# Two receiving buffers for the transposed rows and a single pair of operands, in a mixture-of-experts tail of an fp32 transformer layer

## The reference

```python
def ffn(x, gate_w, gate_b, bias, w1, b1, w2, b2):      # x: 2048 x 512, 8 experts, H = 352
    scores = x @ gate_w.T + gate_b + bias
    top_scores, top_idx = top_k(scores, 2)
    gates = softmax(top_scores)
    comb = sum(one_hot(top_idx, 8) * gates[..., None], axis=1)
    h = silu(einsum('td,ehd->teh', x, w1) + b1)
    y = einsum('teh,edh->ted', h, w2) + b2
    return einsum('ted,te->td', y, comb)

x = x + attention(layernorm(x))      # relu(q) (relu(k)^T v), normalised, projected by Wo
x = x + ffn(layernorm(x), ...)
```

## Time and profile before

| | us |
|---|---|
| median of 3 runs | 1033.69 |
| lowest and highest | 1031.16, 1034.7 |
| the profiled execution | 1031.54 |
| its span, first to last instruction | 1029.7 |
| TensorE busy (share of the span) | 994.1 (97%) |
| VectorE busy | 709.4 (69%) |
| ScalarE busy | 555.8 (54%) |
| GpSimd busy | 247.8 (24%) |
| mean granted clock of TensorE, full speed being 1 | 0.994 |

### The profile page before, as it was taken

How to read it: one execution, slowest core, us unless ns; L and a number is a source line. 1 busy time by engine, 2 the same in 40 slices (tenths; PEclk the granted TensorE clock), 3 DMA queues, 4 the chain that set the end, 5 groups by cost and what they waited for, 6 DMA issues and landing times.

```text
span 1029.7 us, 17472 instructions
## 1 busy us (share of the span) xinstructions
PE 994.1 (97%) x4863; PEld 827.3 (80%) x4864; DVE 709.4 (69%) x1594; ACT 555.8 (54%) x1376; POOL 247.8 (24%) x407
## 2 busy tenths in 40 slices
PE   9999999999999999999999999999999789989897
PEld 7888888888888887887888888888888777777776
DVE  7888655565565677667778878788878655555554
ACT  4545444444444458665555655665557755555443
POOL 1000000000000003314444443344335613323324
PEclk9999999999999999999999999999999989999999
DMA  7102655555444432242111111111148545555654
GB/s 257 37 6 82 219 195 196 192 195 188 163 164 164 164 103 91 85 158 72 52 52 60 62 61 51 51 57 55 51 122 269 136 67 90 97 97 93 99 95 58
DMA packets 121039, 116.01 MB, mean 113 GB/s; under 512 B 47049, under 2 KB 95354, under 8 KB 120866
## 3 DMA queue, kind: packets, MB, share of 16 engines
q1 hardware_dynamic: 111746, 98.51, 31.2%
q0 software_dynamic: 9248, 16.95, 8.7%
HBM read 42.91 MB, written 64.14 MB: 104 GB/s over the span
## 4 chain that ended last, share of the span: by engine, by line
PE 76%; DMA 11%; ACT 4%; issue 2%; SPq 2%; POOL 2%; DVE 2%; ACTq 0%; POOLq 0%; DVEq 0%
PE pK L1691 12%; PE pK L1693 12%; PE pK L1692 12%; DMA xgT<-xr_dram 10%; PE pA L1691 7%; PE pA L1693 7%; PE pA L1692 7%; PE pX L1691 5%; PE pX L1693 5%; PE pX L1692 5%; PE pA L1825 3%; ACT gx L1173 2%; SPq L574 2%; PE pT L1771 2%; PE pT L1706 1%
## 5 line engine op out<-in xcount | busy, mean ns | idle before, releaser
L995 ACT ACTIVATE qs<-q,nrec 128x64 f32<-128x64 f32 x512 | 129.6, 335 | 83.1 <-DVE nrec L1400 82.9
L613 POOL TENSOR_TENSOR wv_lo<-wv_in,wv_hi 128x512 fp32r<-128x512 f32 x4 | 5.2, 1292 | 402.9 <-ACT wo_hi L916 402.9
L1691 PE MATMUL pA<-k_hi,xn_hi 128*128 128x512 f32 x256 | 101.0, 394 | 0.5 <-DVE k_lo L1275 0.5
L1691 PE MATMUL pK<-wq_hi,xnT_hi 128*128 128x512 f32 x256 | 100.4, 392 | 0.0
L1691 PE MATMUL pK<-wk_hi,xnT_hi 128*128 128x512 f32 (+1 forms) x256 | 100.0, 391 | 0.1
L1693 PE MATMUL pK<-wq_hi,xnT_lo 128*128 128x512 f32 x256 | 99.9, 390 | 0.0
L1693 PE MATMUL pA<-k_hi,xn_lo 128*128 128x512 f32 x256 | 99.8, 390 | 0.0
L1692 PE MATMUL pK<-wk_lo,xnT_hi 128*128 128x512 f32 (+1 forms) x256 | 99.8, 390 | 0.0
L1692 PE MATMUL pA<-k_lo,xn_hi 128*128 128x512 f32 x256 | 99.7, 389 | 0.0
L1692 PE MATMUL pK<-wq_lo,xnT_hi 128*128 128x512 f32 x256 | 99.7, 389 | 0.0
L1693 PE MATMUL pK<-wk_hi,xnT_lo 128*128 128x512 f32 (+1 forms) x256 | 99.7, 389 | 0.0
(11 more groups left out here) (289 smaller groups left out, 2486.7 us busy)
## 6 DMA issues: line engine op xcount, KB each, us to landing
xr_dram<-zero SPq DMA_DIRECT2D x10, 3584.0 KB, 12.7
w_in<-in_ffn_w SPq DMA_DIRECT2D x22, 256.0 KB, 4.2
w_in<-in_ffn_w SPq DMA_DIRECT2D x8, 704.0 KB, 6.9
xn<-in_attn_hidden_states SPq DMA_DIRECT2D x16, 256.0 KB, 6.3
wv_in<-in_attn_Wv SPq DMA_DIRECT2D x16, 256.0 KB, 2.8
wo_in<-in_attn_Wo SPq DMA_DIRECT2D x16, 256.0 KB, 3.0
wk_in<-in_attn_Wq SPq DMA_DIRECT2D x4, 1024.0 KB, 5.4
xnT_dram<-xnT SPq DMA_DIRECT2D x4, 1024.0 KB, 12.2
```

The source lines that it names most:

```text
L995: i = nc.scalar.activation(qs[:, s], q[:, s], ACT.Copy, scale=nrec[:, b * HC + h:b * HC + h + 1])
L1691: nc.tensor.matmul(dst, lhs[0], rhs[0], start=start, stop=False)
```

## The change

`xgT` becomes two buffers, taken in turn, each with its own semaphore; the transpose of tile i now waits for the copies of tile i-2 instead of tile i-1. `gx`, `gT_hi` and `gT_lo` become one each. So gT_hi(i+1) waits for h(i) to end and is ahead of h_in(i) on ScalarE, and the copies gx(i+2) wait for gT_lo(i+1). On VectorE gT_lo(i+1) stands ahead of gx(i+2). The w2 pieces of experts 6 and 7 get other addresses; loading the last one now waits for the rows' scatters. On GpSimd put_b2(6), put_b2(7) and the expert table go ahead of the last four scatters of `put_meta`. On TensorE hT(0) goes ahead of h(1). The first tile's copies and split move forward by two weight steps.

```diff
-             184 * KB, 184 * KB + 5664]
+             W2M + 5 * 5664, W2M + 4 * 5664]
...
-    gT_hi = [sb(f"gT_hi{b}", D, (184 + 4 * b) * KB, F32R) for b in range(2)]
-    gT_lo = [sb(f"gT_lo{b}", D, (186 + 4 * b) * KB, F32R) for b in range(2)]
-    gx = [sb(f"gx{b}", D, (186 + 4 * b) * KB) for b in range(2)]
+    gx = sb("gx", D, 189 * KB)
+    gT_hi = sb("gT_hi", D, 191 * KB, F32R)
+    gT_lo = sb("gT_lo", D, 193 * KB, F32R)
-    xgT = sb("xgT", 2 * D, M0 + 1024, U16)
+    xgT = [sb("xgT0", 2 * D, M0 + 1024, U16), sb("xgT1", 2 * D, 184 * KB, U16)]
...
             sp.wait_ge(w_sub_put, W1_SUBS)
-            for e in range(6, E):
-                load_w2(e)
+            load_w2(6)
 
             def load_tile(i):
-                if i >= 1:
-                    sp.wait_ge(rec_lo, i)
-                    sp.wait_ge(rec_hi, i)
+                if i == 0:
+                    sp.wait_ge(rows_ready, 1)
+                elif i == 1:
+                    sp.wait_ge(w_put, WSTEPS - HB)
+                else:
+                    sp.wait_ge(rec_lo, i - 1)
+                    sp.wait_ge(rec_hi, i - 1)
...
             sp.wait_ge(s_xr_last, 32)
-            sp.wait_ge(rows_ready, 1)
+            load_w2(7)
...
-            for b in range(2):
-                put_meta(b)
-
+            pool.wait_ge(w_put, W1T)
+            pool.wait_ge(w_sub_put, W1_SUBS)
+            put_b2(6)
+            pool.wait_ge(s_xr, 32 * (NT - 1))
+            pool.wait_ge(s_xr_last, 32)
+            put_b2(7)
...
             pool.tensor_scalar(tile_expert[:, :], padt[:, :], float(E - 1), None, ALU.min).then_inc(experts_ready, 1)
-            pool.wait_ge(w_put, W1T)
-            pool.wait_ge(w_sub_put, W1_SUBS)
-            put_b2(6)
-            put_b2(7)
+            for b in range(2):
+                put_meta(b)
...
             def act_expert(i, b):
+                if not isinstance(i, int) or i + 1 < NS:
+                    act_gT(i + 1)
                 act_h(i, b)
                 if not isinstance(i, int) or i + 2 < NS:
                     act_rec(i + 2, b)
-                    act_gT(i + 2, b)
                 act_silu(i)
...
                 for b in range(2):
+                    dve_gT(2 * h + (b + 1))
                     dve_rec(2 * h + (b + 2), b)
-                    dve_gT(2 * h + (b + 2), b)
                     dve_y(2 * h + (b - 2), b, 16 * h - 16)
                     dve_hT(2 * h + b, b)
...
+            pe_hT(0)
             pe_h(1, 1, expert(1))
-            pe_hT(0)
             pe_hT(1)
```

More of the change, by code:

```diff
@@ L362, in block_kernel @@
         hT_ones = sem("hT_ones")
-        s_xt = sem("s_xt")
+        s_xt = [sem(f"s_xt{b}") for b in range(2)]
         rows_ready = sem("rows_ready")
@@ L1160, in _ @@
             w_act_lo(3)
-            for k in range(6, 43):
+            for k in range(6, 41):
                 w_hi(k)
@@ L1167, in act_rec, with act_gT @@
             def act_rec(i, b):
-                act.wait_ge(s_xt, 16 * i + 16)
-                if isinstance(i, int) and i < 2:
-                    act.wait_ge(w_put, WSTEPS if i else WSTEPS - HB)
-                else:
-                    act.wait_ge(h_put, i - 1)
-                nc.scalar.copy(words(gx[b][:, :])[:, 0, :], planes(xgT)[:, 0, :]).then_inc(rec_lo, 1)
-            def act_gT(i, b):
+                act.wait_ge(s_xt[b], 16 * (i // 2) + 16 if isinstance(i, int) else 8 * i + (16 - 8 * b))
+                if isinstance(i, int) and i == 0:
+                    act.wait_ge(w_put, W1T)
+                    act.wait_ge(w_sub_put, W1_SUBS)
+                else:
+                    act.wait_ge(gT_lo_ready, i)
+                nc.scalar.copy(words(gx[:, :])[:, 0, :], planes(xgT[b])[:, 0, :]).then_inc(rec_lo, 1)
+            def act_gT(i):
                 act.wait_ge(rec_hi, i + 1)
                 act.wait_ge(rec_lo, i + 1)
-                nc.scalar.copy(gT_hi[b][:, :], gx[b][:, :]).then_inc(gT_hi_ready, 1)
+                if not (isinstance(i, int) and i == 0):
+                    act.wait_ge(h_put, i)
+                nc.scalar.copy(gT_hi[:, :], gx[:, :]).then_inc(gT_hi_ready, 1)
             def act_h(i, b):
                 act.wait_ge(h_put, i + 1)
-                if not (isinstance(i, int) and i == 0):
+                if isinstance(i, int) and i == 0:
+                    act.wait_ge(w_put, WSTEPS - HB)
+                else:
                     act.wait_ge(hT_put, i)
@@ L1200, in act_expert @@
                     act_rec(i + 2, b)
-                    act_gT(i + 2, b)
                 act_silu(i)
-            w_hi(43)
             act_rec(0, 0)
-            act_gT(0, 0)
-            w_hi(44)
-            w_hi(45)
+            w_hi(41)
+            act_gT(0)
+            for k in range(42, WSTEPS):
+                w_hi(k)
             act_rec(1, 1)
-            act_gT(1, 1)
             act.wait_ge(experts_ready, 1)
@@ L1622, in dve_rec, with dve_gT @@
             def dve_rec(i, b):
[L1623 to L1630 removed]
+                dve.wait_ge(s_xt[b], 16 * (i // 2) + 16 if isinstance(i, int) else 8 * i + (16 - 8 * b))
+                if isinstance(i, int) and i == 0:
+                    dve.wait_ge(w_put, W1T)
+                    dve.wait_ge(w_sub_put, W1_SUBS)
+                else:
+                    dve.wait_ge(gT_lo_ready, i)
+                v.tensor_copy(words(gx[:, :])[:, 1, :], planes(xgT[b])[:, 1, :]).then_inc(rec_hi, 1)
+            def dve_gT(i):
                 dve.wait_ge(gT_hi_ready, i + 1)
[L1632 removed]
+                lo(gT_lo[:, :], gx[:, :], gT_hi[:, :]).then_inc(gT_lo_ready, 1)
             def dve_hT(i, b):
@@ L1648, in _ @@
             dve_rec(0, 0)
-            w_lo(43)
-            dve_gT(0, 0)
-            w_lo(44)
+            w_lo(41)
+            dve_gT(0)
+            for k in range(42, WSTEPS):
+                w_lo(k)
             dve_rec(1, 1)
-            w_lo(45)
-            dve_gT(1, 1)
             hT_fill()
@@ L2033, in pe_h @@
                 for n in range(FB):
-                    last = three(h_bank[b], two((gT_hi[b], gT_lo[b]), n * P, P), two((w1_hi, w1_lo), e * H + n * EH, H),
+                    last = three(h_bank[b], two((gT_hi, gT_lo), n * P, P), two((w1_hi, w1_lo), e * H + n * EH, H),
                                  n == 0, n == FB - 1)
```

25 lines of the change are left out of this document (14 added, 11 removed).

## The result

| | before | after |
|---|---|---|
| median, us | 1032.43 (4 runs) | 1023.06 (4 runs) |
| lowest and highest | 1030.8, 1034.7 | 1021.55, 1023.18 |
| ratio, 95% interval | | 0.9904 [0.988, 0.9929] |
| span of the profiled execution | 1029.7 | 1021.5 |
| h(3) / h(38), first matmuls | 834.51 / 1015.57 | 837.06 / 1007.33 |

The forecast was 1013.5 us, range 1006 to 1022. The direction came out as written, the size did not: the gain is 9.4 us by the medians and 8.2 by the two spans. The spans split it: the start loses 2.55 (forecast 0.7), the 35 steps gain 10.8 (forecast 20.9), the tail nothing. So the missing 12 us are 10.1 in the steady part and 1.9 at the start.

What follows compares the result with a forecast made beforehand. The loop of transpose, copy and SyncE's load through the single xgT was taken as the bound. Steady part saves 20.9, start loses 0.7: 20.2 off the median 1033.69 gives 1013.5 us, range 1006 to 1022.

Steps and rivals of the forecast that it cites:

- the start: Start of the expert tiles: later put_meta scatters delay after_ready and tile 1's pe_h; 0.7 us lost on the slower side.
- the 35 steps: Steady part, pe_h of tile 3 to tile 38: 181.06 us falls to 160.2, saving 20.9 us.
- the tail: From pe_h of tile 38 to the end, 14.1 us: same instructions and waits, no change.
- The sum of 5.2: Old steady period per tile: transpose 3.38, copy 0.79 and SyncE's load 1.04, a loop closed by the single xgT.
- New path h(i), gT_hi, h_in: Steady part after the change: single gT buffers make gT_hi wait for pe_h's end; 3.29 us from pe_h's start through h_in.
- Add 1.10 or 1.51: Gap from h_in's end to the next pe_h, inside the body or across the loop's end; steps of 4.39 and 4.80.
- The 0.41 of the loop's end: TensorE's gap after h_in is 1.51 across the loop's end against 1.10 inside the body.
- (b): Rival: adds into out become the next limit by stalling VectorE; steps about 4.95, 1021 to 1027 us; chance 0.14.
- (a): Rival: TensorE runs back to back, the 1.10 and 1.51 shrinking; steps 4.34, gain 28.5, 1005 us; chance 0.10.
- (c): Rival: transposes and adds in flight together stretch each other, transposes taking 9.2; slower, 1046 us; chance 0.04.
- (d): Rival: late silu delays gT_hi, so the new chain is as long as the old, 5.1 to 5.2; 1034 us; chance 0.05.

Runs made afterwards that it cites:

- e7: Kernel before the change with only TensorE's loop turned, so the next tile's expert is loaded ahead of the wait for h_in; ratio to before 0.9994, 35 steps 178.73 us.
- e2: Changed kernel without the 39 indirect adds of y into out and the waits for them; ratio to before 0.9801, 35 steps 159.23 us.
- e1: Changed kernel with TensorE taking expert 0 for every tile, its expert register loads left out; ratio to before 0.9744, 35 steps 152.12 us.
- e3: Changed kernel with TensorE's loop turned, so the next tile's expert is loaded ahead of the wait for h_in; ratio to before 0.9762, 35 steps 153.13 us.
- e6: Changed kernel with the four put_meta scatters issued right behind put_b2(7), ahead of the expert table; ratio to before 0.9862, 35 steps 170.73 us.
- e4: Changed kernel with three extra iotas on GpSimd ahead of each add but the last two, delaying the adds; ratio to before 0.9852, 35 steps 163.31 us.

## Why the prediction was right in direction and wrong in size

**Bound of the kernel before: right, but not taken to its cause.** e7 confirms that the loop of the transposes set the period. Each term was read as a fixed cost, though the row gave SyncE's load as 1.04, and its own line ranges from 0.267 to 1.045. The sum of 5.2 also fits the mean period by luck: it leaves out about 0.4 of SyncE's other instructions, and the turn of the loop it was read from, transpose 898.82 to transpose 904.45, took 5.63.

**New path h(i), gT_hi, h_in: right.** 35 times from h's start to h_in's end sum to 113.2 us in after, 3.24 each, against 3.29. gT_hi starts 0.04 to 0.11 after the end of h, and xgT is off the path.

**The failed step: "Add 1.10 or 1.51".** The gap from h_in's end to the next h was held constant, from a stretch where it had been 1.10. In after the 17 gaps inside the body average 1.41 and the 18 others 1.84; all 35 together are 57.0 us. The forecast had 19 x 1.10 + 16 x 1.51 = 45.1. That is 11.9 too few, less 1.9 for the 3.24: the 10.1 that are missing, but for rounding. e2 (159.23) shows it to be the adds, e1 and e3 (152.12, 153.13) show that it acts by this load. The forecast moved TensorE's load onto the path, took the load at its shortest, and did not look at the load's own line, where the kernel before already had 302 as the median and 997 as the longest:

```profile
L2065 PEldq TENSOR_LOAD <-tile_expert x70: 296/302/997, 834.1 to 1014.7; - x70
```

The long ones among these stand ahead of a y. The 35 ahead of an h took 0.30 to 0.31 each, since they began between 0.6 before and 0.5 after an add's start, or over 4 after one. So the 1.10 was read truly; what did not carry over is the load's place in time against the adds. In the changed kernel 28 of the 35 begin 1.9 to 3.0 after an add's start.

The two can even lock together. h(24) at 938.42 leads to y(22) and to its add at 944.46, that add holds the load behind h_in(25), and so h(26) is at 948.56: 10.14 for two tiles, where the sum has 9.19. (The add's row names a DMA as what released it, but y(22) ended at 943.68, and 24 of the 27 adds of tiles 10 to 36 start 0.78 to 0.82 after their y ends, as this one does.)

**The 0.41 of the loop's end.** The forecast took it as the loop's own cost. With adds away it stays (e2: gaps of 1.17 and 1.47 on average); with the load away it is gone (e1: 1.16 and 1.08), and with the load ahead of the wait as well (e3: 1.08 across the loop's end). TensorE's sequencer in e2 tells why. The load takes 0.30 to 0.31 in both places, but starts mostly 0.15 to 0.18 after h_in's end inside the body and 0.53 across the loop's end, behind the loop's branch and its register operations:

```profile
L2068 PEldq COMPARE_BRANCH  x17: 76/208/218, 845.6 to 991.6; - x17
```

So the time does belong to the loop's end, and it counts only where a load and the address arithmetic on it stand behind it. In e1 the same branch, again 208 at the median, lies under matmuls that are already queued.

The forecast set the Trainium skill's figure of about 51 ns for an always-taken branch (Advanced Engine Details and Errata, Control Flow Timing) against this row. The loop ends in a compare-and-branch, for which the same section of the Trainium skill gives about 108 ns; the 208 measured here is nearly twice that. The Trainium skill also states a floor of about 600 ns for a `tensor_load` (DMA: Bandwidth & Descriptors, Latency and other measured facts). The runs here show 296 to 314 ns for it in SBUF with no add near, so as a floor it doesn't hold in this kernel.

**Start: right in sign, 1.9 short.** The last put_meta was at 812.78 instead of 811.3, of which 1.2 was there before any changed instruction. From there to the gather it was 819.07 - 812.78 = 6.3, where 4.8 had been used. The last scatter landed after 5.5 (4.8 is the median of the group before), and GpSimd began the gather 0.8 after the landing, a term that the sum did not have. add_after followed within 5.7 instead of 6.9. Together h(1) came at 825.66, forecast 823.8. From there h(2) took 5.9 (5.7 was forecast) and h(3) 5.5 (4.4 to 6.0 in the forecast), at half clock for most of it:

```profile
826.00:829.50 3.50, 3.50 (x12) 3.09 (x11) 1.21 (x3) 1.39 (x5) 0.00 (x0) 0.50 0.30 68
829.50:833.00 3.50, 2.36 (x9) 1.93 (x9) 1.47 (x3) 2.53 (x6) 0.00 (x0) 0.50 0.04 7
```

0.50 is the lower of TensorE's two levels, 1.2 GHz, granted after the engine had been busy for only 1.29 us of the four from 822 to 826. e6 puts the price of the scatters' new place at 2.6 us of h(3), so here the sign of this part of the change is settled: it costs.

**The rivals.** (b), the adds as the next limit, had the size nearly right by luck, 4.95 a step against 4.87 measured, but by a way that did not happen: VectorE waited for an add once, 1.6 us. (a), steps of 4.34, is what the kernel does once the load is off the path (e3: 4.38 on average); its condition, that the 1.10 and 1.51 shrink by themselves, was not met. (c): the transposes landed in 3.0/3.3/5.2 (min, median, max) against 3.0/3.2/4.3 and cost nothing. (d) is excluded by the 3.24.

## What to carry to other kernels

Look at each instruction that a change puts on the path by its own line, with its minimum, median and maximum, and not by the one duration next to it: a load with 302 as its median and 997 as its longest is no constant, and where its short ones were read matters as much as how short they were. Read registers as early as the order allows, ahead of the wait that ends last and not behind it; here that is worth 17.1 us of 170.3 and costs no instruction. When a stage's time is a loop of several terms, ask of each why it is longer than its shortest, before counting the whole loop as saved.

## What the hardware showed that I had not expected

A register load from SBUF takes 0.27 to 0.32 us on SyncE, ScalarE and TensorE with no indirect add about, and up to 1.05 (SyncE), 1.07 (ScalarE) and 1.18 (TensorE, in e4) with them. In the kernels with full adds nearly all loads of over 400 ns ended 2.3 to 3.5 us after an add's start (a few up to 4.0, two at 1.4). Such a load shows as "issue" ahead of the next instruction and not as a wait for anything.

Delaying the adds behind useless work made the kernel faster (e4), by 7.0 us over the 35 steps. In this kernel a periodic DMA meets a periodic load, and an edit that moves one against the other can gain or lose several us by that alone. An edit that moves both together (e6) does not.
